# Gathered rows of the routed experts: spreads issued by SyncE six tiles ahead, lists loaded twelve ahead with 32 places

## The chip, the core and the metric

The kernel runs on one core of one Trainium2 chip. The metric is the device time of one execution in microseconds (us). Timed three times, the kernel before took 3968.76 us in the median (3964.9 to 3973.75). The core has five engines with an instruction stream each: TensorE (PE, matrix products), VectorE (DVE), ScalarE (ACT), GpSimd (POOL) and SyncE (SP). They meet at semaphores. 16 DMA engines move data for all of them.

## The reference

Two layers are chained, and the input is added at the end. The first is a modulated linear layer on 8 x 1024 rows of 512 (8192 tokens). The second is a feed-forward layer with a shared part (512 to 1024 to 512) and a routed part. The routed part is what the change touches:

```
topk_idx, w = _route(xf, router_w, e_bias)      # 8 of 64 experts for each token
order = argsort(topk_idx.reshape(-1)); tok = order // K
sorted_x = xf[tok]                               # 65536 rows, grouped by expert
g = ragged_dot(sorted_x, gate_w, group_sizes)    # [512 x 256] of the expert of the row
u = ragged_dot(sorted_x, up_w, group_sizes)
o = ragged_dot(silu(g) * u, down_w, group_sizes) # [256 x 512]
routed = zeros.at[tok].add(o * w)                # weighted and added into the token's row
out = x + shared + routed                        # x is the layer's first input
```

## The kernel before

A first phase (to about 1460 us) computes the linear layer, the shared part and the routing for all tokens. It writes the rows to be gathered into `y_rows` in DRAM, lists of (row, weight) for each expert, and a table with one entry per routed tile.

The second phase is a loop over routed tiles. A tile is 128 (token, expert) pairs of one expert; there are 532 tiles here, four to a turn of the loop (`UN = 4`). An expert's weights are a set of three DMAs of 512 KB: gate, up and down. Only the first tile of an expert brings a set, by a branch on a bit of the table. An expert takes from one tile to some dozens, and experts are ordered so that a small one stands beside a large one. Every product is made of three in fp32r (high x high, high x low, low x high), so weights and activations are split into a high and a low part: ScalarE makes the high, VectorE the low.

What happens to tile j, and on which engine:

- SyncE loads its list (`load_list`, a 1 KB DMA; `lists` has 16 places in turn) and, with `weights`, its expert's set.
- VectorE copies the row numbers out of the list (`rows_from`, tile j+8 in step j).
- GpSimd gathers 128 rows by an indirect DMA (`gather`, tile j+7 in step j) into `x_rows`, and later adds the result rows to the output by an indirect DMA (`scatter`, tile j-3 in step j, behind the gather of its step).
- ScalarE issues the "spread" of a pair of tiles (`spread`, in even steps, pair j+4, j+5): four DMAs of 128 KB that rearrange `x_rows` into `x_split`, from which a 32 x 32 transpose gives the columns that TensorE needs. Both buffers hold two pairs.
- VectorE transposes (`turn_x`, tile j+3 in step j), ScalarE and VectorE split (`x_high`, `x_low`), TensorE computes gate and up (line 1231), then turns the hidden rows of tile j-1 (line 1240), and computes down of tile j-2 (line 1249).
- ScalarE scales and copies the result out (`weigh`, first thing in step j, tile j-3). With `start_weights` and `end_weights` it makes the high parts of a new set for tile j+2 in step j; VectorE makes the low parts (`weights_low`) behind it, in steps j and j+1.

Each engine takes its instructions in the order in which the code is written, so a wait holds all that stands behind it. SyncE loads the list of tile n and then the set of tile n-4. What paces it is the 16 places: `load_list(n)` waits for the scatter of tile n-16 to have landed. It thus has nothing in front of a set but one list. The DMAs of SyncE and of ScalarE go out on a queue each, those of GpSimd on a third.

The sets have four places each (`RAW`, `RING`), and a set's issue waits for the set before it to have landed (`raw_gu_ld`, `raw_d_ld`, lines 1132 to 1135).

Of the kernel before, what the change touches and what calls it, by code (L numbers as in the profile page):

```python
# [16 lines left out]
P = 128  # L17
# [15 lines left out]
def build(nc, x, cond, cw, cbias, aff_w, aff_b, router_w, e_bias, gate_w, up_w, down_w,  # L33
          sh_gate, sh_up, sh_down, out):
    B, L, C = x.shape
    N = B * L
# [15 lines left out]
    UN = 4  # L52
# [20 lines left out]
    with top:  # L73
# [950 lines left out]
        with ExitStack() as tmp:  # L1024
# [6 lines left out]
            raw = [sb("raw_gu", [P, RAW, KC, 2 * H]), sb("raw_d", [P, RAW, KH, C])]  # L1031
            wgu = [sb("w_gu_h", [P, RING, KC, 2 * H], F32R, LINE), sb("w_gu_l", [P, RING, KC, 2 * H], F32R, LINE)]
            wdn = [sb("w_dn_h", [P, RING, KH, C], F32R, LINE), sb("w_dn_l", [P, RING, KH, C], F32R, LINE)]
            LISTS = 16
            lists = sb("lists", [P, LISTS, 2], I32)
            from_row = [sb(f"from_row{n}", [P, 1], I32) for n in range(UN)]
            to_row = [sb(f"to_row{n}", [P, 1], I32) for n in range(UN)]
# [29 lines left out]
            PARTS = [(True, 0, KC // 2 + 1), (True, KC // 2 + 1, KC), (False, 0, KH)]  # L1067
            NTURN = MAXT // UN
            assert MAXT % UN == 0 and NTURN > 2
            AHEAD = UN  # L1070

            def field(eng, j, f, top_val):

# [33 lines left out]
            @blk.sync  # L1107
            def _(sp):
                sp.dma_start(trow[:], table.rearrange("(a j) f -> a (j f)", a=1)).then_inc(tab_ld, 16)
                sp.wait_ge(tab_ld, 16)  # L1110

                def load_list(j, u, g):
                    known = isinstance(j, int)
                    if not known or j >= UN:
                        sp.wait_ge(list_ld[u], 16 * g)
                    if not known or j >= LISTS:
                        sp.wait_ge(added[u], 16 * (g - (LISTS // UN - 1)))
                        sp.nop(nofuse=True)
                    off = field(sp, j, 0, LROWS - P)
                    sp.dma_start(entry(j, 0, 2), slots[bass.ds(off, P), :]).then_inc(list_ld[u], 16)  # L1120

                def weights(j, is_first):

                    with sp.If(is_first > 0):
                        order = field(sp, j, 1, E)
                        e = field(sp, j, 2, E - 1)
                        half = order & (RAW - 1)
                        sp.wait_ge(split, 3 * order + 1)
                        sp.nop(nofuse=True)
                        if not isinstance(j, int) or j > 0:  # L1130

                            sp.wait_ge(raw_gu_ld, 32 * order)
                            sp.nop(nofuse=True)
                            sp.wait_ge(raw_d_ld, 16 * order)
                            sp.nop(nofuse=True)
                        for n, w in enumerate((gate_w, up_w)):
                            sp.dma_start(raw[0][:, bass.ds(half, 1), :, n * H:(n + 1) * H].rearrange("p a k n -> p (a k) n"),
                                         w[bass.ds(e, 1)].rearrange("e (k p) h -> p (e k) h", p=P)).then_inc(raw_gu_ld, 16)
                        sp.dma_start(raw[1][:, bass.ds(half, 1), :, :].rearrange("p a k n -> p (a k) n"),
                                     down_w[bass.ds(e, 1)].rearrange("e (k p) h -> p (e k) h", p=P)).then_inc(raw_d_ld, 16)  # L1140

                def step(g, u, is_first):
                    n = g * UN + u
                    load_list(n, u, g)
                    weights(n - AHEAD, is_first)

                for n in range(UN):
                    load_list(n, n, 0)
                    if n == 1:
                        weights(0, field(sp, 0, 3, 1))  # L1150
                for n in range(UN, 2 * UN):
                    load_list(n, n - UN, 1)
                for n in range(1, UN):
                    weights(n, field(sp, n, 3, 1))
                for n in range(2 * UN, LISTS):
                    load_list(n, n % UN, n // UN)
                    weights(n - AHEAD, field(sp, n - AHEAD, 3, 1))
                last_turn = field(sp, 0, 5, NTURN - 1)
                sp.wait_ge(words, 1)
                with sp.Fori(LISTS // UN, NTURN + 2) as g:  # L1160
                    with sp.If(last_turn >= g - 2):
                        turn = Turn(sp, g - 1)
                        for u in range(UN):
                            step(g, u, turn.first(u))
                for u in range(UN):
                    sp.wait_ge(list_ld[u], 16 * last_turn + 48)
                    sp.nop(nofuse=True)

            @blk.gpsimd
            def _(pool):  # L1170
# [24 lines left out]

                def step(g, u):
                    j = g * UN + u
                    gather(g + 1 + (u + 3) // UN, (u + 3) % UN)
                    if not isinstance(j, int) or j >= 3:
                        scatter(j - 3, (u - 3) % UN, g - 1 if u < 3 else g)  # L1200

                pool.wait_ge(tab_ld, 16)
                for n in range(UN + 3):
                    gather(n // UN, n % UN)
                for u in range(UN):
                    step(0, u)
# [7 lines left out]
                for u in range(1, UN):  # L1214
                    scatter(UN * last_turn + u, u, last_turn)
                for u in range(UN):
                    pool.wait_ge(x_ld[u], 16 * last_turn + (48 if u < 3 else 32))
                for u in range(UN):
                    pool.wait_ge(added[u], 16 * last_turn + 16)

# [61 lines left out]
            def _(act):  # L1282
# [49 lines left out]
                def spread(j, v, g):  # L1332

                    for u in (2 * v, 2 * v + 1):
                        act.wait_ge(x_ld[u], 16 * (g + 1))
                        act.nop(nofuse=True)
                    if not isinstance(j, int) or j >= UN:
                        act.wait_ge(dve_turned, j - 2)
                        act.nop(nofuse=True)
                    for a in range(QD):  # L1340
                        act.dma_start(x_split[v][a * SQ:(a + 1) * SQ, :, :, :].rearrange("c i u e -> c (i u) e"),  # L1341
                                     xg[v][:, :, a * P:(a + 1) * P]).then_inc(x_moved[v], 16)

                def step(g, u, turn):
                    j = g * UN + u
                    known = isinstance(j, int)
# [7 lines left out]
                        h_high(j - 1, (u - 1) % UN)  # L1354
                    with act.If(turn.first(u + 2) > 0):
                        end_weights(turn.order(u + 2))
                    if u % 2 == 0:
                        spread(j + UN, u // 2, g + 1)

                spread(0, 0, 0)  # L1360
                spread(2, 1, 0)
                act.wait_ge(words, 1)
                start_weights(None, 0)
                end_weights(0)
# [24 lines left out]
            def _(dve):  # L1389
# [85 lines left out]
                turn_x(1, 1, 0)  # L1475
                x_low(1, 1)
                turn_x(2, 2, 0)
                turn = Turn(dve, 0)
                with dve.If(turn.first(1) > 0):
                    weights_low(turn.order(1), (0,))  # L1480
# [40 lines left out]
```

## Time and profile before

| | |
|---|---|
| median of three timed runs | 3968.76 us |
| profiled execution: its time / its span | 3965.72 us / 3964.0 us |
| PE busy | 3733.3 us, 94% of the span, x17024 |
| DVE / ACT / POOL busy | 2235.7 / 1495.3 / 1946.4 us |
| mean granted TensorE clock | 0.977 of full speed |
| routed stretch, 1500 to 3964 us | DMA engines 0.87 busy |

The profile shows one execution. Its time outside the span is 1.7 us. A line of a timeline gives the start in microseconds from the beginning of the span, the length, the engine (SPq and ACTq are the instruction queues of SyncE and ScalarE, where DMAs are issued), the line of the program and what it writes and reads. The chain of waits is followed back from the last instruction, each piece being what released the next. The clock column is the mean of two levels, 1 being 2.4 GHz and 0.5 being 1.2 GHz.

### The profile page before, as it was taken

The page shows a single profiled execution, that of the slowest core. Times are in us where ns is not written, and L with a number is a line of the kernel's source. Part 1 is how long each engine was busy: PE and PEld are TensorE (multiplying, and loading weights), DVE is VectorE, ACT ScalarE, POOL GpSimd, SP SyncE. Part 2 cuts the span into 40 slices and gives each one's busy share as a digit, 9 for nine tenths or more (in the row PEclk, how much of TensorE's full clock was granted, in tenths as well). Part 3 has the DMA queues.
Part 4 walks back from the last instruction along what each step waited for, and adds up shares of the span by engine and source line. Part 5 has one row for each costly group of instructions (what it writes and reads, how often), then busy time and mean ns, then how long its engine had stood idle before and what let it go on. Part 6 is the DMA issues. An engine that isn't in the chain of part 4 may idle for free.

```text
span 3964.0 us, 91393 instructions
## 1 busy us (share of the span) xinstructions
PE 3733.3 (94%) x17024; PEld 3040.4 (77%) x17025; DVE 2235.7 (56%) x4612; ACT 1495.3 (38%) x3339; POOL 1946.4 (49%) x1601
## 2 busy tenths in 40 slices
PE   7999999999999959999999999999999999999987
PEld 5877877878787848878878878787878778777775
DVE  4655555555555645555555555555555555566554
ACT  3222222222222214444444444444444444444443
POOL 1453333333333425655556556555656555555554
PEclk9999999999999979999999999999999999999998
DMA  5121112112111228888889888988888898899887
GB/s 181 51 57 44 44 54 54 44 44 65 44 44 54 44 70 181 182 196 177 177 191 184 182 189 182 200 176 188 178 190 185 187 201 175 194 204 204 198 185 158
DMA packets 589051, 550.56 MB, mean 139 GB/s; under 512 B 133625, under 2 KB 443265, under 8 KB 588929
## 3 DMA queue, kind: packets, MB, share of 16 engines
q0 software_dynamic: 136112, 281.38, 36.5%
q10 hardware_dynamic: 291584, 140.58, 13.9%
q1 hardware_dynamic: 161234, 127.04, 11.7%
q8 instruction: 70, 1.15, 0.2%
q14 instruction: 51, 0.42, 0.1%
HBM read 229.07 MB, written 179.19 MB: 103 GB/s over the span
## 4 chain that ended last, share of the span: by engine, by line
PE 46%; DMA 7%; issue 4%; ACTq 3%; DVE 2%; SPq 1%; DVEq 1%; ACT 1%; POOLq 0%; POOL 0%
PE bank L1231 30%; PE bank L1249 14%; DMA x_split<-x_rows 4%; PE bank L1240 2%; ACTq L1341 2%; DMA raw_d<-in_L_ffn_down_w_dram 1%; DMA out_dram<-o_rows,to_row 1%; DVE w_dn_l L30 1%; DMA lists<-slot_list 1%; DMA x_rows<-y_rows,from_row 1%; DVE x_cols L1407 0%; ACTq L1074 0%; SPq L1074 0%; ACT x_h L1289 0%; DVE w_gu_l L30 0%
## 5 line engine op out<-in xcount | busy, mean ns | idle before, releaser
L1193 POOL DMA_INDIRECT out_dram<-o_rows,to_row x532 | 879.5, 1653 | 278.2 <-issue 230.0
L1177 POOL DMA_INDIRECT x_rows<-y_rows,from_row x539 | 543.9, 1009 | 840.6 <-DMA x_split<-x_rows 605.5
L428 POOL DMA_INDIRECT slot_list<-ent,pos x512 | 503.9, 984 | 862.7 <-PE bank L454 385.4
L1231 PE MATMUL bank<-w_gu_h,x_h 128*128 x2128 | 844.3, 397 | 86.1 <-DVE x_l L30 42.7
L1231 PE MATMUL bank<-w_gu_h,x_l 128*128 x2128 | 840.3, 395 | 0.0
L1231 PE MATMUL bank<-w_gu_l,x_h 128*128 x2128 | 839.7, 395 | 0.0
L1407 DVE STREAM_TRANSPOSE x_cols<-x_split 128x512 f32<-128x512 f32 x535 | 580.1, 1084 | 293.9 <-DMA x_split<-x_rows 293.2
L1414 DVE TENSOR_TENSOR e_hf<-bank,e_sg 128x256 f32<-128x256 f32 x532 | 225.2, 423 | 684.4 <-ACT e_sg L1295 366.2
L1231 PEld LDWEIGHTS bank<-w_gu_h,x_h 128*128 128x128 f32 x2128 | 406.4, 191 | 186.4 <-issue 99.1
L1249 PE MATMUL bank<-w_dn_h,e_h_h 128*128 x1064 | 468.1, 440 | 33.7 <-DVE e_h_l L30 20.5
L1231 PEld LDWEIGHTS bank<-w_gu_l,x_h 128*128 128x128 f32 x2128 | 406.9, 191 | 86.7
L1231 PEld LDWEIGHTS bank<-w_gu_h,x_l 128*128 128x128 f32 x2128 | 406.7, 191 | 86.9
L1249 PE MATMUL bank<-w_dn_h,e_h_l 128*128 x1064 | 425.6, 400 | 0.0
L1249 PE MATMUL bank<-w_dn_l,e_h_h 128*128 x1064 | 424.1, 399 | 0.0
L1309 ACT COPY to_row<-lists 128x1 int32 (+1 forms) x532 | 102.7, 193 | 842.9 <-issue 657.4
L30 DVE TENSOR_TENSOR x_l<-x_cols,x_h 128x512 fp32r<-128x512 f32 x534 | 368.7, 690 | 46.4 <-issue 12.7
L1289 ACT CAST x_h<-x_cols 128x512 fp32r<-128x512 f32 x534 | 329.4, 617 | 103.9 <-DVE x_cols L1407 94.9
L1310 ACT ACTIVATE o_rows<-bank,lists 128x512 f32<-128x512 f32 x532 | 366.9, 690 | 0.0
L1295 ACT ACTIVATE e_sg<-bank 128x256 f32<-128x256 f32 x532 | 202.9, 381 | 404.0 <-PE bank L1231 362.8
L1249 PEld LDWEIGHTS bank<-w_dn_h,e_h_h 128*128 128x128 f32 x1064 | 202.7, 190 | 67.5 <-issue 43.8
L742 DVE TENSOR_TENSOR stage_d<-bank,sg 128x512 f32<-128x512 f32 x128 | 88.5, 692 | 277.1 <-PE bank L454 261.9
L656 ACT ACTIVATE sg<-bank 128x512 f32<-128x512 f32 x128 | 76.5, 598 | 428.4 <-PE bank L454 376.5
(242 smaller groups left out, 5946.7 us busy)
## 6 DMA issues: line engine op xcount, KB each, us to landing
x_split<-x_rows ACTq DMA_DIRECT2D x1072, 128.0 KB
xin<-in_x_dram SPq DMA_DIRECT2D x16, 1024.0 KB
y_rows<-yrow SPq DMA_DIRECT2D x64, 256.0 KB
stage_d<-in_x_dram SPq DMA_DIRECT2D x16, 1024.0 KB
out_dram<-stage_d SPq DMA_DIRECT2D x16, 1024.0 KB
raw_gu<-in_L_ffn_gate_w_dram SPq DMA_DIRECT2D x29, 512.0 KB
raw_gu<-in_L_ffn_up_w_dram SPq DMA_DIRECT2D x29, 512.0 KB
raw_d<-in_L_ffn_down_w_dram SPq DMA_DIRECT2D x29, 512.0 KB
```

Source lines behind the costliest of these rows:

```text
L30: return nc.vector.tensor_tensor(out, full, high.bitcast(F32), ALU.subtract)
L428: nc.gpsimd.indirect_dma_start(slots, bass.IndirectOffsetOnAxis(ap=pos[v][:, t, k:k + 1], axis=0), ent[v][:, t, k, :], None).then_inc(scat ...
L1177: nc.gpsimd.indirect_dma_start(xg[u // 2][:, u % 2, :], None, y_rows, bass.IndirectOffsetOnAxis(ap=from_row[u][:].bitcast(U32), axis=0)).t ...
L1193: nc.gpsimd.indirect_dma_start(out, bass.IndirectOffsetOnAxis(ap=to_row[u][:].bitcast(U32), axis=0), og[u][:], None, compute_op=ALU.add).t ...
L1231: last = nc.tensor.matmul(b_gu[u % 2][:], xp[a][:, u % 2, k, :], wgu[b][:, bass.ds(place, 1), k, :].rearrange("p a n -> p (a n)"), start=( ...
L1249: last = nc.tensor.matmul(b_o[u % 2][:], hp[a][:, u % 2, k, :], wdn[b][:, bass.ds(place, 1), k, :].rearrange("p a n -> p (a n)"), start=(k ...
L1289: nc.scalar.copy(xp[0][:, u % 2, :, :], x_cols[:]).then_inc(act_x, 1)
L1295: nc.scalar.activation(sg[:, u % 2, :], b_gu[u % 2][:, 0:H], ACT.Silu).then_inc(act_gu, 1)
L1309: nc.scalar.copy(to_row[u][:], entry(j, 0, 1))
L1310: nc.scalar.activation(og[u][:], b_o[u % 2][:], ACT.Copy, scale=entry(j, 1, 2).bitcast(F32)).then_inc(act_do, 1)
L1407: nc.vector.transpose(x_cols[:].rearrange("p k (c i) -> p k i c", i=QD), x_split[u // 2][:, :, u % 2, :].rearrange("p i (k r) -> p k i r", ...
L1414: nc.vector.tensor_tensor(hf[:, u % 2, :], b_gu[u % 2][:, H:2 * H], sg[:, u % 2, :], ALU.mult).then_inc(dve_gu, 1)
```

## The change

Four things are moved in the routed phase. SyncE instead of ScalarE issues the spreads, in even steps, of pair j+6, j+7 instead of j+4, j+5. They stand in front of the list of that turn. SyncE's steps are numbered anew: in step j it issues the spread, the list of tile j+12 (was n, beside set n-4, so 4 tiles between the two; now 6) and the set of tile j+6. `lists` has 32 places instead of 16. GpSimd gathers tile j+8 instead of j+7 in step j, and VectorE copies the row numbers of tile j+9 instead of j+8. The transfers, the arithmetic and the buffers of rows are the same.

```diff
-            LISTS = 16
+            LISTS = 32
-            AHEAD = UN
+            LIST_AHEAD, SPREAD_AHEAD, LOAD_AHEAD = 12, 6, 6
@@ SyncE
+                def spread(j, v, g):
+
+                    for u in (2 * v, 2 * v + 1):
+                        sp.wait_ge(x_ld[u], 16 * (g + 1))
+                        sp.nop(nofuse=True)
+                    if not isinstance(j, int) or j >= UN:
+                        sp.wait_ge(dve_turned, j - 2)
+                        sp.nop(nofuse=True)
+                    for a in range(QD):
+                        sp.dma_start(x_split[v][a * SQ:(a + 1) * SQ, :, :, :].rearrange("c i u e -> c (i u) e"),
+                                     xg[v][:, :, a * P:(a + 1) * P]).then_inc(x_moved[v], 16)
-                def step(g, u, is_first):
-                    n = g * UN + u
-                    load_list(n, u, g)
-                    weights(n - AHEAD, is_first)
+                def step(g, u, turn):
+                    j = g * UN + u
+                    if u % 2 == 0:
+                        spread(j + SPREAD_AHEAD, (u + SPREAD_AHEAD) % UN // 2, g + (u + SPREAD_AHEAD) // UN)
+                    load_list(j + LIST_AHEAD, (u + LIST_AHEAD) % UN, g + (u + LIST_AHEAD) // UN)
+                    weights(j + LOAD_AHEAD, turn.first(u + LOAD_AHEAD - UN))
@@ GpSimd
-                    gather(g + 1 + (u + 3) // UN, (u + 3) % UN)
+                    gather(g + 2, u)
@@ ScalarE
-                    if u % 2 == 0:
-                        spread(j + UN, u // 2, g + 1)
@@ VectorE
-                    rows_from(j + 2 * UN, u, g + 2)
+                    rows_from(j + 2 * UN + 1, (u + 1) % UN, g + 2 + (u + 1) // UN)
```

The first tiles, before the loop, are written out anew to match: SyncE issues the first three spreads between its first lists and sets.

SyncE, in the loop over turns, one odd and one even step (before): `lists` and `raw_gu`, `raw_d` are the list and the set.

```order
L1124 UNCONDITIONAL_BRANCH
L1074 ISA
L1074 TENSOR_LOAD trow
L1074 ISA x2
L1120 REGISTER_ALU
L1120 ISA
L1120 DMA lists<-slot_list 128x2
L1124 REGISTER_ALU x2
L1124 COMPARE_AND_BRANCH
L1074 ISA
L1074 TENSOR_LOAD trow
L1074 ISA x3
L1074 TENSOR_LOAD trow
```

The same place in the kernel after, from the end of an odd step on:

```order
L1137 UNCONDITIONAL_BRANCH
L1129 REGISTER_ALU
L1132 DMA x_split<-x_rows 32x8x128 x4
L1074 ISA
L1074 TENSOR_LOAD trow
L1074 ISA x2
L1121 REGISTER_ALU
L1121 ISA
L1121 DMA lists<-slot_list 128x2
L1137 REGISTER_ALU x2
L1137 COMPARE_AND_BRANCH
```

The four spread DMAs now stand between the branch over one set and the next list, on the queue that carries the sets.

ScalarE, end of an even step of the loop, before (`e_h_h` is the hidden part's high half, `o_rows` the result rows of the next step):

```order
L1329 ISA
L1315 ISA
L1315 COPY w_dn_h<-raw_d 128x1024
L1355 UNCONDITIONAL_BRANCH
L1341 DMA x_split<-x_rows 32x8x128 x4
L1306 ISA
L1309 REGISTER_ALU
L1309 ISA
L1309 COPY to_row<-lists 128x1
L1310 ISA
L1310 ACTIVATE o_rows<-bank,lists 128x512
```

and after:

```order
L1342 COPY w_gu_h<-raw_gu 128x512
L1356 ISA
L1342 ISA
L1342 COPY w_dn_h<-raw_d 128x1024
L1370 UNCONDITIONAL_BRANCH
L1333 ISA
L1336 REGISTER_ALU
L1336 ISA
L1336 COPY to_row<-lists 128x1
L1337 ISA
L1337 ACTIVATE o_rows<-bank,lists 128x512
```

The spread has gone from between the set's casts and the next step's `to_row` and `o_rows`.

## Rows read from the trace of the kernel before

**Rows 1.** Windows: engines busy (x instructions), PEclk, DMA share, GB/s, by stretch

```profile
1500.00:3964.00 2464.00, 2342.04 (x10518) 1894.12 (x10516) 1414.90 (x2715) 1096.72 (x2718) 1406.86 (x1057) 0.98 0.87 187
...
1739.26:1776.00 36.74, 28.57 (x121) 22.02 (x120) 20.91 (x37) 17.78 (x38) 18.35 (x13) 0.95 0.95 230
...
2539.00:2551.00 12.00, 12.00 (x58) 9.81 (x57) 6.22 (x12) 6.17 (x16) 6.98 (x5) 1.00 1.06 275
```

**Rows 2.** Windows of line 1231 alone (gate and up products), same stretches

```profile
1500.00:3964.00 2464.00, 1546.44 (x6300) 1199.90 (x6300) 0.98 0.87 187
...
1739.26:1776.00 36.74, 17.60 (x72) 13.47 (x72) 0.95 0.95 230
2510.53:2573.25 62.72, 37.23 (x145) 28.60 (x145) 0.92 0.92 212
```

**Rows 3.** Chain of waits, 2084 to 2111: start, length, what

```profile
2084.11 2.73 PE bank L1231 x12
...
2097.11 2.73 PE bank L1231 x12
```

**Rows 4.** Timeline of SyncE, 1715 to 1756: start, length, instruction

```profile
1715.06 21.08 SPq L1120 DMA_DIRECT2D lists<-slot_list  x6
1739.77 0.40 SPq L1137 DMA_DIRECT2D raw_gu<-in_L_ffn_gate_w_dram  x1
...
1750.85 0.39 SPq L1137 DMA_DIRECT2D raw_gu<-in_L_ffn_gate_w_dram  x1
...
1753.43 2.06 SPq L1120 DMA_DIRECT2D lists<-slot_list  x2
```

**Rows 5.** Timeline of SyncE, 2512 to 2580

```profile
2517.29 17.62 SPq L1120 DMA_DIRECT2D lists<-slot_list  x5
2539.46 0.01 SPq L1137 DMA_DIRECT2D raw_gu<-in_L_ffn_gate_w_dram  x1
...
2551.67 0.39 SPq L1137 DMA_DIRECT2D raw_gu<-in_L_ffn_gate_w_dram  x1
```

**Rows 6.** Timeline of TensorE at four places

```profile
1752.10 0.39 PE L1231 MATMUL bank<-w_gu_h,x_h 128*128 x1
...
1776.00 0.50 PE L1231 MATMUL bank<-w_gu_h,x_h 128*128 x1 [1.02 <-DVE w_dn_l L30]
...
2523.37 0.39 PE L1231 MATMUL bank<-w_gu_h,x_h 128*128 x1
...
2549.37 0.39 PE L1231 MATMUL bank<-w_gu_h,x_h 128*128 x1
```

**Rows 7.** Timeline of ScalarE, 1750 to 1778 and 2512 to 2580

```profile
1762.31 1.48 ACT L1315 CAST w_gu_h<-raw_gu  x1 [1.59 <-issue]
...
1766.88 1.48 ACT L1315 CAST w_gu_h<-raw_gu  x1
...
2518.99 2.01 ACTq L1341 DMA_DIRECT2D x_split<-x_rows  x3
...
2563.05 1.47 ACT L1315 CAST w_gu_h<-raw_gu  x1 [1.03 <-issue]
```

**Rows 8.** Chain of waits, 1735 to 1757 and 2512 to 2580

```profile
1744.89 10.33 DMA x_split<-x_rows
...
2541.13 10.23 DMA raw_d<-in_L_ffn_down_w_dram
```

**Rows 9.** Timeline of VectorE, 1750 to 1778 and 2512 to 2580

```profile
1755.24 1.08 DVE L1407 STREAM_TRANSPOSE x_cols<-x_split 128x512 f32<-128x512 f32 x1 [6.63 <-DMA x_split<-x_rows]
...
2528.23 1.07 DVE L1407 STREAM_TRANSPOSE x_cols<-x_split 128x512 f32<-128x512 f32 x1
...
2561.03 0.15 DVE L1397 COPY from_row<-lists 128x1 int32 x1 [1.89 <-DMA lists<-slot_list]
```

**Rows 10.** DMA by queue, 1500 to 3964: packets, MB, share

```profile
q1 hardware_dynamic: 112640, 44.62, 7.4%
```

**Rows 11.** Who waited for whom, 1500 to 3964: total, times, longest

```profile
DVE x_cols L1407 <- DMA x_split<-x_rows: 291.2, 214, 7.6
```

More of the change, by code:

```diff
@@ L1120, in load_list @@
                     sp.dma_start(entry(j, 0, 2), slots[bass.ds(off, P), :]).then_inc(list_ld[u], 16)
+                def spread(j, v, g):
[4 more added lines that the diff above has]
+                        sp.wait_ge(dve_turned, j - 2)
+                        sp.nop(nofuse=True)
+                    for a in range(QD):
+                        sp.dma_start(x_split[v][a * SQ:(a + 1) * SQ, :, :, :].rearrange("c i u e -> c (i u) e"),
+                                     xg[v][:, :, a * P:(a + 1) * P]).then_inc(x_moved[v], 16)
                 def weights(j, is_first):
@@ L1150, in _ @@
                         weights(0, field(sp, 0, 3, 1))
+                spread(0, 0, 0)
                 for n in range(UN, 2 * UN):
                     load_list(n, n - UN, 1)
-                for n in range(1, UN):
+                    if n == UN + 1:
+                        spread(2, 1, 0)
+                for n in range(1, LOAD_AHEAD):
                     weights(n, field(sp, n, 3, 1))
-                for n in range(2 * UN, LISTS):
+                for n in range(2 * UN, LIST_AHEAD):
                     load_list(n, n % UN, n // UN)
-                    weights(n - AHEAD, field(sp, n - AHEAD, 3, 1))
+                spread(UN, 0, 1)
+                sp.wait_ge(words, 1)
+                known = (LISTS - LIST_AHEAD) // UN
+                assert known < N * TOPK // (P * UN)
+                for g in range(known):
+                    turn = Turn(sp, g + 1)
+                    for u in range(UN):
+                        step(g, u, turn)
                 last_turn = field(sp, 0, 5, NTURN - 1)
[L1159 to L1162, printed above, removed]
+                with sp.Fori(known, NTURN) as g:
+                    with sp.If(last_turn >= g):
+                        turn = Turn(sp, g + 1)
                         for u in range(UN):
-                            step(g, u, turn.first(u))
+                            step(g, u, turn)
                 for u in range(UN):
-                    sp.wait_ge(list_ld[u], 16 * last_turn + 48)
+                    sp.wait_ge(list_ld[u], 16 * last_turn + 16 * (1 + LIST_AHEAD // UN))
+                    sp.nop(nofuse=True)
+                for v in range(UN // 2):
+                    sp.wait_ge(x_moved[v], 16 * QD * last_turn + 16 * QD * (3 - v))
                     sp.nop(nofuse=True)
@@ L1202, in _ @@
                 pool.wait_ge(tab_ld, 16)
-                for n in range(UN + 3):
+                for n in range(2 * UN):
                     gather(n // UN, n % UN)
@@ L1216, in _ @@
                 for u in range(UN):
-                    pool.wait_ge(x_ld[u], 16 * last_turn + (48 if u < 3 else 32))
+                    pool.wait_ge(x_ld[u], 16 * last_turn + 48)
                 for u in range(UN):
@@ L1330, in end_weights @@
                     weights_high(order, order & (RAW - 1), order & (RING - 1), 2)
[L1332 to L1342, printed above, removed]
                 def step(g, u, turn):
@@ L1356, in step @@
                         end_weights(turn.order(u + 2))
-                    if u % 2 == 0:
-                        spread(j + UN, u // 2, g + 1)
-                spread(0, 0, 0)
-                spread(2, 1, 0)
                 act.wait_ge(words, 1)
@@ L1477, in _ @@
                 turn_x(2, 2, 0)
+                rows_from(2 * UN, 0, 2)
                 turn = Turn(dve, 0)
```

## The prediction

> **What bounds the kernel now.** I read the windows first. Between 1500 and 3964 us the DMA engines are 0.87 busy and TensorE is busy 2342 of 2464 us [rows 1]. The same stretch with line 1231 alone has 6300 products [rows 2], 12 to a tile, so 525 tiles. The chain of waits in a quiet place has nothing in it but TensorE: 2084.11 to 2097.11 is three tiles in 13.00 us, 4.333 us each [rows 3]. 525 tiles at that pace are 2275 us, so 189 us of the stretch are lost. That is all a change to the feeding of the tiles can win.
>
> It is lost at the weight sets. Gate and up of a set are issued 28 times after 1500 us; 26 of these come in pairs whose second follows the first by 10 to 20 us. Two pairs are in rows 4 and 5. Around the first, 72 products of line 1231 (6 tiles, 26.0 us at pace) take 36.74 us; around the second, 145 (12 tiles, 52.0 us) take 62.72 us [rows 2]. Each pair loses 10.7 us, 13 pairs 139 us. The other 50 us are the last tiles and small gaps.
>
> What ends last in a pair is the spread. The one issued last at 1744.89 takes 10.33 us [rows 8], VectorE stands 6.63 us before its transpose at 1755.24 [rows 9], and in the whole stretch such waits sum to 291 us in 214 places, up to 7.6 us [rows 11]. Meanwhile the set is in flight: from 1739.77 to 1750.85, when SyncE, which waits for it, issues the next [rows 4]. That is 11.1 us (12.2 in the second pair, rows 5). The sets themselves are early: the first set's cast on ScalarE is at 1762.31, 22.5 us after its issue [rows 7]. After the second set's cast starts it takes 9.1 us until TensorE starts its tile (1766.88 to 1776.00; 10.2 in the second pair, from 2563.05 to the end of its window at 2573.25), with the low parts on VectorE ending it [rows 6, 7]. So a pair has two causes: late spread (and list, 1.89 us at 2561.03, rows 9), and casts.
>
> **The change part by part.** I call t(j) the time at which TensorE starts gate and up of tile j.
>
> Spread. Today ScalarE issues it at the end of step j for tile j+4, whose transpose is in VectorE's step j+1. SyncE will issue it for tile j+6 as soon as tile j+3 is transposed. That is t(j)+5.9: TensorE started a tile at 2523.37 and the transpose of its step ended at 2528.23+1.07 [rows 6, 9]. It is needed at t(j+3)+4.9, so it gets 12.0 us. Four issues take 2.7 (3 of them 2.01 on ScalarE, rows 7) and waking 0.3, leaving 9.0 us for the move. The 10.33 us case is then late by 1.3 us instead of 5 to 6. On its own this would take away most of the stall of a pair's first tile. In quiet stretches TensorE loses nothing now [rows 3], so nothing comes back there.
>
> ScalarE is rid of 2.7 us of issue per pair of tiles. It is busy 1097 of 2464 us [rows 1], so I count 0 (bounds 0 to 2.7 us per pair of sets).
>
> Lists. 32 places remove SyncE's wait for a scatter; 1 KB each. The list of tile j+12 is used in VectorE's step j+3, about 13 us later. It costs nothing.
>
> Sets. This is what speaks against it. SyncE's queue was paced by the scatters and ran early enough to give the first set 22.5 us (12.2 in the other pair). Now the set of tile m is issued in step m-6, behind the spread that waits for the transpose in VectorE's step. For even m: 5.9 + 3.0 for the spread + 1.7 for the list (two lists in 2.06 us, less one issue of 0.36, rows 4) + 4.1 from the list to the set (3.6 from 1736.14 to 1739.77, 4.55 from 2534.91 to 2539.46, rows 4, 5) = t(m-6)+14.7, which is t(m-2)-2.6. For odd m one more list, but a tile earlier: t(m-7)+16.4 = t(m-2)-5.3. In the second pair today it is 2539.46 against 2549.37 [rows 5, 6], t(m-2)-9.9. So sets go out 5 to 20 us later than now, and ScalarE wants gate and up of the set at about t(m-2)+2.
>
> The second set of a pair waits for the first to land: +11.1 (rows 4). Its gate and up land later by, I estimate, 6.5 us (two thirds of a set's 11.1 is 7.4; less, since TensorE stands and the tiles' own traffic thins). Then 9.1 to the start of its tile. Together t(m+1) = issue + 26.7. At pace it would be t(m-2)+13.0. The loss is 26.7-2.6-13.0 = 11.1 us for even m, 26.7-5.3-13.0 = 8.4 for odd, mean 9.75. Spread and list of the next tiles come in SyncE's order behind the second set, and they land at about the time it does, so they hide behind it. Against 10.7 that is 0.95 gained, times 13 = 12 us.
>
> Outside the pairs I give 6 us for the small gaps that follow a pair while the stream of gathers is thin, and for the two lone sets (0 to 25 by the 50 us above). Bounds of the terms: set in flight 9.5 to 13; cast to start 8 to 10.2; issue of the set up to 4.3 us (one tile) later if SyncE runs behind. 13 pairs make of each 1 us 13 us: the sum lies between -60 and +50.
>
> The queue. Of the 7.4% of DMA time on SyncE's queue [rows 10] nearly all are sets. VectorE stands for a list of 1 KB at 2561.03 while the second set, issued from 2551.67 on, has just been in flight [rows 5, 9]: a list behind a set comes late, so the queue serves about in order. The spreads now join it, and the one of pair j+8 stands behind the set of tile j+7, as counted above.
>
> The Trainium skill, page "DMA: Bandwidth & Descriptors", section "Issuing engines are not separate DMA queues", says that issuing from several engines saves only the sequencer's issue time, as all DMAs run on the same 16 engines. Taken alone, the move would then matter by the 2.7 us of issue only. The section "Queues, rings and completion order" of the same page says that SP and ACT each own a row of rings, and each ring is consumed in order while the engine goes round the rows. By this the spread loses its own turn beside a set. The trace's list behind the set speaks for the second.
>
> Sum: 3965.7 (profiled execution) - 18 = 3947.7 us. The median of the runs shown is 3.0 above it, so 3950 us.
>
> **Rivals.**
>
> A. The sets arrive in time, and only casts are left. For: TensorE's windows with a set in flight are full (2539 to 2551: 12.00 of 12 busy, DMA engines over full at 1.06, 275 GB/s, rows 1), so bytes do get through; with two queues instead of three in play a set may land in 8 rather than 11. Then a pair costs what it takes from the first cast to the start of the second set's tile, 1762.31 to 1776.00 [rows 6, 7], less two tiles at pace: 13.7-8.7 = 5.0 us. 13 x (10.7-5.0) = 74 us: 3895 us. Against: the issue at t(m-2)-2.6.
>
> B. The wait moves from the spread to the set (slower). Place: ScalarE's `start_weights` of the first set and, behind it, the second, whose issue waits for the first. It decides at one point: a pair costs 10.7 when the first set is issued at t(m-2)-3.0 (26.7-13.0-10.7). My mean is 0.95 before it. If SyncE is held longer, by a gather that lands after the transpose (`x_ld` stands in front of the set too) or by its own code, by one tile, the loss is 14.05: 13 x 3.35 = +44 us, 4010 us. For: everything now stands in one queue of instructions. Against: SyncE mostly waits now (five lists in 17.62 us, 4.3 apart, rows 5, against 1.7 when free, rows 4).
>
> C. SyncE itself becomes the bound. Four tiles are 17.3 us; two spreads 6.0, four lists 6.8, the turn's word about 1.1: 13.9. Over 17.3 each microsecond costs 131 (525 tiles in fours). One over is 4100 us. The margin is 3.4 us, a quarter.
>
> D. Nothing measurable: what the spread gives the set takes, within 8 us: 3969 us.
>
> **How the numbers follow.** The forecast, 3930 to 3960, has 0.38; A with what lies between 0.17; B 0.25; C 0.04; D 0.16. Three runs of this kernel lie 9 us apart, so about 0.2% (8 us) is what a measurement can tell from no change. Faster by more: most of the forecast (0.35) and A, 0.52. Same: D and the edge, 0.17. Slower: B, C and the rest, 0.31. The range reaches to A's price and to B's: 3890 to 4012 us; the forecast's own is 3930 to 3960.
>
> **What would show it.** Right: the wait for `x_split` before the transposes falls from 291 us to under 100; ScalarE's idle time before the cast of `w_gu_h` is ended by the DMA of `raw_gu`, 3 to 6 us a pair; a first set is issued 2 to 6 us before t(m-2); pairs lose 8 to 11 us; 4.33 us a tile between pairs; SyncE waits for VectorE's transpose. Wrong: first sets issued more than 8 us before t(m-2) (A), or after it (B); tiles over 4.4 us in quiet stretches (C); transposes still waiting 5 us in pairs.

## The result, and the profile after

The changed kernel takes 4025.35 us, the median of 4 runs (4012.24 to 4048.41); the kernel before 3969.4 us, the median of 4. The ratio is 1.0147, with a 95% interval of 1.0099 to 1.0195. It is slower by about 56 us; the forecast was 3950 us, and the range ended at 4012. The profiled execution is the slowest of the four: its span is 4046.7 us against 3964.0 before, so its sums explain 82.7 us, more than the medians differ by.

The windows of the stretch with the routed tiles, columns as in [rows 1]:

```profile
1500.00:4046.00 2546.00, 2365.96 (x10520) 1898.80 (x10518) 1418.86 (x2715) 1124.64 (x2719) 1415.22 (x1057) 0.97 0.88 181
```

TensorE has the same work in 82 us more, and is busy for 24 us more of them (2342.0 before): the last section comes back to these. What the engines waited for in it, from the waits of SyncE, then VectorE, then ScalarE (waiting line, what ended the wait, total us, times, longest):

```profile
SPq L1127 <- DMA x_rows<-y_rows,from_row: 28.2, 26, 3.9
SPq L1148 <- DMA raw_d<-in_L_ffn_down_w_dram: 12.6, 10, 3.4
SPq L1146 <- DMA raw_gu<-in_L_ffn_up_w_dram: 1.0, 2, 0.8
SPq L1119 <- DMA out_dram<-o_rows,to_row: 0.8, 1, 0.8
SPq L1130 <- DVE x_cols L1418: 0.7, 1, 0.7
```

```profile
DVE e_hf L1425 <- ACT e_sg L1322: 615.7, 332, 9.6
DVE from_row L1408 <- DMA lists<-slot_list: 203.7, 131, 3.8
```

```profile
ACT w_gu_h L1342 <- DMA raw_gu<-in_L_ffn_up_w_dram: 122.3, 26, 8.2
```

The 291.2 us before the transposes [rows 11] have gone: no wait for `x_split` is left in VectorE's list. In their place VectorE waits 203.7 us for lists of 1 KB, and ScalarE, for the first time, 122.3 us for sets. The row to read first is a small one. SyncE waits 43 us in 2546 for everything together. In the kernel before it waited for scatters:

```profile
SPq L1118 <- DMA out_dram<-o_rows,to_row: 804.5, 388, 7.2
```

An engine that issues all day and waits for nothing is itself what the others wait for. The chain of the page says the same. By engine, before:

```profile
PE 46%; DMA 7%; issue 4%; ACTq 3%; DVE 2%; SPq 1%; DVEq 1%; ACT 1%; POOLq 0%; POOL 0%
```

After, by engine and by line:

```profile
PE 20%; SPq 19%; issue 12%; DMA 10%; POOLq 1%; DVE 1%; POOL 1%; DVEq 0%; ACT 0%; another core or an unknown queue 0%; ACTq 0%
PE bank L1258 13%; SPq L1132 7%; PE bank L1276 7%; SPq L1074 5%; DMA out_dram<-o_rows,to_row 4%; SPq L1121 3%; DMA x_split<-x_rows 3%; DMA raw_d<-in_L_ffn_down_w_dram 2%; DMA x_rows<-y_rows,from_row 1%; PE bank L1267 1%; DMA lists<-slot_list 1%; SPq L1137 1%; SPq L1085 1%; SPq L1150 1%; POOLq L1074 0%
```

SyncE's timeline in a quiet place, with no set near, shows two turns of four tiles (start, length, instruction):

```profile
2663.16 2.55 SPq L1132 DMA_DIRECT2D x_split<-x_rows  x4
2668.31 2.58 SPq L1121 DMA_DIRECT2D lists<-slot_list  x2
2671.93 2.23 SPq L1132 DMA_DIRECT2D x_split<-x_rows  x4
2675.97 2.79 SPq L1121 DMA_DIRECT2D lists<-slot_list  x2
2682.52 2.11 SPq L1132 DMA_DIRECT2D x_split<-x_rows  x4
2686.01 2.17 SPq L1121 DMA_DIRECT2D lists<-slot_list  x2
2688.79 2.65 SPq L1132 DMA_DIRECT2D x_split<-x_rows  x4
2693.38 3.88 SPq L1121 DMA_DIRECT2D lists<-slot_list  x2
2701.98 1.92 SPq L1132 DMA_DIRECT2D x_split<-x_rows  x4
```

A turn begins at 2663.16, 2682.52 and 2701.98: 19.4 and 19.5 us, where TensorE needs 17.33 for four tiles. SyncE waits 0.8 us in these 39; from the end of a spread at 2665.71 to the first list at 2668.31, for instance, SyncE runs its guards and reads one field of the table. Over the stretch from 1500 to 3900 a turn is 19.2 us in the mean (18.5 median). Summed by what its instructions belong to, SyncE's 2400 us there are, for each of 125 turns:

| part of a turn | measured, us | in the prediction |
|---|---|---|
| four lists | 8.1 | 6.8, with the checks |
| four checks whether a tile brings a set | 1.9 | in the lists' 6.8 |
| two spreads (with 0.2 of waiting) | 6.9 | 6.0 |
| the sets' reads and issues, spread over all turns | 1.0 | not counted |
| the turn's word | 0.75 | 1.1 |
| the loop's own branches | 0.64 | not counted |
| sum | 19.2 | 13.9 |

The checks belong to the lists in the prediction, because its 1.7 us a list is the pitch from one list to the next [rows 4], and a check that finds no set lies between those two.

Then the sets. One pair, from SyncE's timeline:

```profile
2584.73 0.68 SPq L1150 DMA_DIRECT2D raw_gu<-in_L_ffn_gate_w_dram  x1
...
2595.28 0.39 SPq L1150 DMA_DIRECT2D raw_gu<-in_L_ffn_gate_w_dram  x1
```

TensorE's timeline (in brackets the idle time ahead and what ended it):

```profile
2584.01 0.40 PE L1258 MATMUL bank<-w_gu_h,x_h 128*128 x1
...
2588.47 0.39 PE L1258 MATMUL bank<-w_gu_h,x_h 128*128 x1
...
2593.97 0.44 PE L1267 MATMUL bank<-ident,e_hf 128*128 128x128 f32 x2 [2.62 <-DVE e_hf L1425]
2597.26 0.79 PE L1276 MATMUL bank<-w_dn_h,e_h_h 128*128 x1 [2.86 <-DVE e_h_l L30]
...
2601.49 0.79 PE L1258 MATMUL bank<-w_gu_h,x_h 128*128 x1 [1.30 <-DVE w_dn_l L30]
```

ScalarE's and VectorE's:

```profile
2591.61 1.47 ACT L1342 CAST w_gu_h<-raw_gu  x1 [6.21 <-DMA raw_gu<-in_L_ffn_up_w_dram]
...
2601.68 1.47 ACT L1342 CAST w_gu_h<-raw_gu  x1 [4.86 <-DMA raw_gu<-in_L_ffn_up_w_dram]
```

```profile
2593.49 0.42 DVE L1425 TENSOR_TENSOR e_hf<-bank,e_sg 128x256 f32<-128x256 f32 x1 [6.31 <-ACT e_sg L1322]
...
2596.33 0.15 DVE L1408 COPY from_row<-lists 128x1 int32 x1 [1.73 <-DMA lists<-slot_list]
```

The first set's tile starts at 2601.49; its set was issued at 2584.73, 0.7 us after the tile two ahead had started (2584.01). ScalarE stands 6.21 us for it with the current tile's `e_sg` behind the cast, VectorE stands for `e_sg` and then 1.73 us for a list. The tile at 2588.47 takes 13.0 us, and with the two behind it (next starts 2611.20 and 2617.28) the pair costs 15.8.

I split the time that TensorE loses against 4.333 us a tile, from the start of the first tile to that of the last, into what is lost around the sets (from four tiles before the first set's to three after the second's, 13 pairs and the lone set of tile 526) and the rest, in each profiled execution. It is used in the table after the experiments. From before to after: around sets 150.8 to 175.5 us, elsewhere 9.4 to 67.3. The sum rises by 82.6, and the spans differ by 82.7.

### The profile page after: what moved, and what is told of

It reads as the page before. It is cut to its first block, busy times and chain, and to the rows that moved or that the text cites. A ratio compares the mean times of both kernels' runs of the same rounds, so it can differ in the third digit from the quotient of the medians.

```text
span 4046.7 us, 92175 instructions
## 1 busy us (share of the span) xinstructions
PE 3757.7 (93%) x17024; PEld 3044.6 (75%) x17025; DVE 2239.1 (55%) x4613; ACT 1523.0 (38%) x3339; POOL 1959.2 (48%) x1602
## 4 chain that ended last, share of the span: by engine, by line
PE 20%; SPq 19%; issue 12%; DMA 10%; POOLq 1%; DVE 1%; POOL 1%; DVEq 0%; ACT 0%; another core or an unknown queue 0%; ACTq 0%
PE bank L1258 13%; SPq L1132 7%; PE bank L1276 7%; SPq L1074 5%; DMA out_dram<-o_rows,to_row 4%; SPq L1121 3%; DMA x_split<-x_rows 3%; DMA raw_d<-in_L_ffn_down_w_dram 2%; DMA x_rows<-y_rows,from_row 1%; PE bank L1267 1%; DMA lists<-slot_list 1%; SPq L1137 1%; SPq L1085 1%; SPq L1150 1%; POOLq L1074 0%
## 5 line engine op out<-in xcount | busy, mean ns | idle before, releaser
L1204 POOL DMA_INDIRECT x_rows<-y_rows,from_row x540 | 554.3, 1027 | 898.3 <-DMA x_split<-x_rows 517.4
L1267 PE MATMUL bank<-ident,e_hf 128*128 128x128 f32 x1064 | 204.2, 273 | 38.6 <-DVE e_hf L1425 31.7
L1276 PEld LDWEIGHTS bank<-w_dn_h,e_h_l 128*128 128x128 f32 x1064 | 204.7, 192 | 46.3
```

Source lines behind the costliest of these rows:

```text
L1204: nc.gpsimd.indirect_dma_start(xg[u // 2][:, u % 2, :], None, y_rows, bass.IndirectOffsetOnAxis(ap=from_row[u][:].bitcast(U32), axis=0)).t ...
L1267: last = nc.tensor.transpose(b_h[u % 2][:, k * P:(k + 1) * P], hf[:, u % 2, k * P:(k + 1) * P], ident[:])
L1276: last = nc.tensor.matmul(b_o[u % 2][:], hp[a][:, u % 2, k, :], wdn[b][:, bass.ds(place, 1), k, :].rearrange("p a n -> p (a n)"), start=(k ...
```

## The experiments

Theory 1: the changed kernel is held by SyncE's own issuing time. The rivals: sets go out too late in the program (B of the prediction); 1 KB lists come late because they share a queue with sets of 1.5 MB and spreads; the early spread itself is of no use. Which theory is number 2 or 3 differs from one expectation to the next; each says it.

**One more read on SyncE.** The changed kernel with

```diff
                     if u % 2 == 0:
                         spread(...)
+                    field(sp, j, 0, LROWS - P)
                     load_list(j + LIST_AHEAD, ...)
```

> The kernel after, with one more read of a table field on SyncE in each step of its loop (value not used), about 1 us by the trace of after (13 reads of a field with their asserts take about 12.5 us). Theory 1 (SyncE's own instructions are the bound: a turn of four tiles took 19.2 us in the mean from spread to spread in the trace of after, and 17.3 us is TensorE's pace): four more us a turn come in full, 131 turns, +350 to +600 us, about 4450 us. Theory 2 (the weight sets are issued too late, in SyncE's order behind the spread): SyncE has slack between, and only the sets move, by up to 4 us a pair: +20 to +60 us, about 4060. Theory 3 (the lists land late because they stand behind 512 KB of spread in one queue): nearly no change, since the order in the queue is the same: 0 to +40.

4237.65 us (4223.42 to 4246.36), ratio 1.0687 [1.0647, 1.0728]. The turn grew from 19.2 to 20.7 us; 131 turns make of 1.5 us 197 us, and 212 were measured. One read a tile that nobody uses costs 212 us (5.4% by the ratios): this is the bound. The time lies outside all three ranges, between theory 1's (350 us and more) and those of theories 2 and 3 (at most 60). Theory 1 had the mechanism and too high a size: the four reads take 3.8 us of a turn in this trace, but the lists beside them take less than they did (6.8 instead of 8.1), and so do the checks. Why they do isn't shown.

**The lists on ScalarE.** The changed kernel, SyncE with spreads and sets only:

```diff
@@ SyncE, step
-                    load_list(j + LIST_AHEAD, (u + LIST_AHEAD) % UN, g + (u + LIST_AHEAD) // UN)
@@ ScalarE, end of the step
+                    load_list(j + LIST_AHEAD, (u + LIST_AHEAD) % UN, g + (u + LIST_AHEAD) // UN)
```

> The kernel after, with the lists of the loop loaded by ScalarE at the end of its step (12 ahead as before) instead of by SyncE, so SyncE has spreads and sets only. Theory 1: SyncE is rid of some 9 us a turn and has room again; the small losses between the pairs go (about 80 us) and the sets go out earlier: 3900 to 3960 us. Theory 2: SyncE's steps still start with the wait for the transpose, the sets are as late as now: pairs still lose 10 to 11 us, about 3960 to 3990. Theory 3: the lists have a queue of their own, VectorE's wait for lists (204 us) goes, about 3950 to 3990. Theories 1 and 3 are told apart by the first kernel of this call.

3899.01 us (3896.58 to 3903.38), ratio 0.9846 [0.9817, 0.9875]: better than both kernels, by the ratios 1.5% under the kernel before and 3.0%, 119 us, under the changed one, at the lower edge of theory 1's range. SyncE's waits:

```profile
SPq L1127 <- DMA x_rows<-y_rows,from_row: 622.9, 219, 6.0
SPq L1148 <- DMA raw_d<-in_L_ffn_down_w_dram: 25.4, 12, 3.9
SPq L1130 <- DVE x_cols L1424: 21.1, 35, 1.7
```

SyncE now waits 623 us for gathered rows. The sets stand behind that wait, but it costs nothing that earlier sets would give back: further down they go out earlier, and nothing is gained. VectorE's wait for lists is gone, its wait for `x_split` is 11.9 us, ScalarE's for sets 41.2. So the change without the load of the lists on SyncE is worth 61 us over the kernel before. Spreads and sets still share a queue here, and GpSimd and VectorE keep their new order, so none of these is what cost the changed kernel its time. How much of the 61 us is the earlier spread and how much is ScalarE's relief from issuing it was not separated.

**Only the 32 places,** in the kernel before:

```diff
-            LISTS = 16
+            LISTS = 32
```

> The kernel before with 32 places for lists instead of 16 and nothing else. SyncE is then no longer held by scatters of 16 tiles back and issues sets as early as their four places allow. If late sets or late lists are part of what a pair of sets costs in the kernel before, it is faster, by up to 3 us a pair (3930 us); if the late spread is what costs, no change: 3969 within 8 us.

3974.23 us (3966.37 to 3985.17), ratio 1.0028 [1.0011, 1.0046]. The places alone give nothing. Sets then go out some 88 us ahead of the tile two before theirs, and the tiles lose 186 us in sum instead of 160 (the profiled span is only 9 us longer, as its first routed tile starts 15 us earlier), so sets that are early in flight are no gain by themselves.

**The spread early, but from ScalarE,** the kernel before with 32 places and

```diff
-                    if u % 2 == 0:
-                        spread(j + UN, u // 2, g + 1)
+                    if u % 2 == 1:
+                        spread(j + 5, (u + 5) % UN // 2, g + (u + 5) // UN)
@@ GpSimd
-                    gather(g + 1 + (u + 3) // UN, (u + 3) % UN)
+                    gather(g + 2, u)
```

> The kernel before with 32 places for lists and the spreads still issued by ScalarE, but one step earlier: at the end of odd step k for the pair k+5, k+6 (was: even step j, pair j+4, j+5), with the gathers one tile earlier to match. It has the earlier spread without any load on SyncE and without the shared queue. If the early spread is worth something and SyncE's load is what spoilt it (theory 1), a pair loses 5 to 8 us instead of 10.7: 3895 to 3940 us. If the earlier spread gives nothing because the casts and the sets bound a pair anyway: 3969 within 8 us.

3983.19 us (3976.51 to 3993.43), ratio 1.0057 [1.0037, 1.0078]. The transposes' wait falls to 27.6 us, but not the time: it is 0.3% over that of the 32 places alone and above both expected ranges. One place of ScalarE's timeline shows what stands against the gain:

```profile
1962.09 0.37 ACT L1304 CAST e_h_h<-bank 128x256 fp32r<-128x256 f32 x1
1966.64 2.70 ACTq L1344 DMA_DIRECT2D x_split<-x_rows  x4
1971.14 0.19 ACT L1312 COPY to_row<-lists 128x1 int32 x1 [8.69 <-DMA lists<-slot_list]
```

ScalarE has nothing running from 1962.5 until it issues the spread at 1966.64, since the spread stands behind the gathers' semaphores; then come 2.70 us of issue, and the tile's own `to_row` and `o_rows` stand behind both. The engine named in brackets is only the last semaphore in line. How much of ScalarE's waiting before `to_row` is of this kind was not summed, so the price of it is argued from this place.

**Giving SyncE its load back without the lists.** The kernel with the lists on ScalarE, with two reads on SyncE before each tile's check for a set:

```diff
+                    field(sp, j, 0, LROWS - P)
+                    field(sp, j, 0, LROWS - P)
                     weights(j + LOAD_AHEAD, turn.first(u + LOAD_AHEAD - UN))
```

> The kernel e2 (lists loaded by ScalarE) with two unused reads of a table field on SyncE ahead of every tile's weight step. This gives SyncE back about the time that the lists took, with no list in its queue. Theory 1 (the changed kernel is held by SyncE's own issuing time): eight reads at about 1 us put 8 us on a turn of four tiles that e2 leaves with 622.9 us of idle waiting over 131 turns (4.8 us a turn); SyncE's turn goes to 18.5 to 19.5 us again, its waits for gathers go under 60 us, and the time to 4000 to 4060 us. Theory 2 (the lists cost because they stand in one queue with the sets and spreads, not because of SyncE's time): 3890 to 3910 us, as e2.

3974.27 us (3965.8 to 3992.66), ratio 1.0012 [0.9993, 1.003]. SyncE's queue holds what it held without the reads, so the 1.66% between the two ratios, 66 us, are SyncE's time alone. That is under theory 1's 4000 to 4060 us and far over theory 2's 3890 to 3910. SyncE's waits for gathers are 49.2 us, as expected, but the point where its time becomes the bound is only just reached. A read took 0.87 us here, so the eight take 7 us of a turn and not 8, and SyncE's own time rises by 5.2 us, as the other instructions again take less.

**Sets two tiles earlier,** first with the lists on ScalarE, then in the changed kernel itself (the turn's word is then read a turn further ahead, which the lines leave out):

```diff
-            LIST_AHEAD, SPREAD_AHEAD, LOAD_AHEAD = 12, 6, 6
+            LIST_AHEAD, SPREAD_AHEAD, LOAD_AHEAD = 12, 6, 8
-                    weights(j + LOAD_AHEAD, turn.first(u + LOAD_AHEAD - UN))
+                    weights(j + LOAD_AHEAD, turn.first(u))
```

> The kernel e2 with the expert sets issued for the tile eight ahead instead of six. The set's slot must still be free (its guard is kept), so the issue comes earlier only where the slot is. Theory 1: of the losses left in e2, the 41.2 us that ScalarE waits for sets go, and the pairs of sets lose less: 3860 to 3895 us. Theory 2 (the sets wait for their slot, not for their place in SyncE's program): no change, 3893 to 3905 us, and the waits of SyncE at the guard of the slot grow.

> The changed kernel with the expert sets issued for the tile eight ahead instead of six, lists still on SyncE. Theory 1 (SyncE's own time is the bound): SyncE's steps do not get shorter, so the turn stays at 18.5 us or more; only the lateness of sets that comes from SyncE's delay goes: ScalarE's 122.3 us of waits for sets shrink, those of VectorE for lists (203.7 us) stay, and the time is 3990 to 4030 us. Theory 2 (what costs in the changed kernel is that sets go out too late in the program, as rival B has it): the gain is most of the 56 us that the change lost and more, 3920 to 3970 us.

With the lists on ScalarE: 3912.42 us (3904.64 to 3916.9), ratio 0.9852 [0.983, 0.9874], no gain, and above both expected ranges. Both theories fail: the sets do leave earlier, 15.3 us before the tile two ahead instead of 6.4, and ScalarE's 41.2 us for them go, but VectorE's wait for `x_split` rises from 11.9 to 52.6 us. In the changed kernel: 4018.58 us (4017.54 to 4031.91), ratio 1.0115 [1.0093, 1.0137], which can't be told from the changed kernel's. This one settles rival B. First sets leave 16.6 us before that tile instead of 0.6, ScalarE's wait for them falls from 122.3 us to 1.8, and the tiles around the sets lose 179.9 us as against 175.5. ScalarE's and VectorE's waits in it:

```profile
ACT w_gu_h L1342 <- DMA raw_gu<-in_L_ffn_up_w_dram: 1.8, 2, 1.0
ACT x_h L1316 <- DVE x_cols L1418: 95.2, 41, 7.2
```

```profile
DVE from_row L1408 <- DMA lists<-slot_list: 279.9, 112, 8.5
```

ScalarE's wait for sets has gone, 120 us. VectorE's for lists has grown by 76, and ScalarE's for VectorE's transposes by 68 (27.6 in the changed kernel).

**Lists four tiles earlier,** the changed kernel with

```diff
-            LIST_AHEAD, SPREAD_AHEAD, LOAD_AHEAD = 12, 6, 6
+            LIST_AHEAD, SPREAD_AHEAD, LOAD_AHEAD = 16, 6, 6
```

> The changed kernel with the lists loaded by SyncE sixteen tiles ahead instead of twelve; SyncE does the same work in the same order. In the changed kernel VectorE waited 203.7 us for lists. Theory 1 (SyncE's issuing time per turn is the bound, and the waits for lists, sets and rows only show who notices it): the waits for lists shrink to under 100 us, those for gathered rows, casts or sets grow in their place, the turn stays at 18.5 us or more, and the time at 4010 to 4040 us. Theory 2 (lists land too late since each stands behind 1.5 MB of a set in SyncE's queue): the 203.7 us go, the time is 3930 to 3985 us.

4051.69 us (4038.76 to 4055.52), ratio 1.0188 [1.0162, 1.0213], a little above theory 1's range and far from theory 2's. VectorE's and ScalarE's waits:

```profile
DVE x_cols L1418 <- DMA x_split<-x_rows: 208.0, 102, 4.6
```

```profile
ACT to_row L1336 <- DMA out_dram<-o_rows,to_row: 217.9, 125, 4.0
ACT to_row L1336 <- PE bank L1276: 169.0, 203, 3.4
ACT w_gu_h L1342 <- DMA raw_gu<-in_L_ffn_up_w_dram: 157.4, 26, 10.5
```

The 203.7 us for lists are gone, and 208.0 for spreads stand there. A list that lands late behind a set is thus not the cause either. Three kernels (the changed one, with earlier sets, with earlier lists) give SyncE the same work for a turn and take about the same time; only the buffer that is waited for differs.

**One read and three,** in the kernel with the lists on ScalarE:

```diff
+                    field(sp, j, 0, LROWS - P)            # once, or three times
                     weights(j + LOAD_AHEAD, turn.first(u + LOAD_AHEAD - UN))
```

> The kernel e2 (lists loaded by ScalarE) with one unused read of a table field on SyncE per tile, 4 of some 0.9 us in a turn of four tiles, where SyncE waits 4.8 us a turn in e2. Theory 1 (SyncE costs nothing until its own time per turn reaches TensorE's, then all of the excess): 3895 to 3915 us, half or less of the step to e5 (3974 us with two reads). Theory 2 (every instruction on SyncE costs its time, whatever the others do): half of the step between e2 and e5, 3930 to 3945 us.

> The kernel e2 with three unused reads of a table field on SyncE per tile. Theory 1 (past the knee each read costs what it cost on top of the changed kernel, 212 us for one per tile): 4140 to 4200 us; two reads and then a third would stand on either side of the changed kernel (4025 us), whose lists are then worth between two and three reads a tile. Theory 2 (a read costs what it cost between e2 and e5, 37 us): 4000 to 4030 us.

One: 3939.63 us (3926.64 to 3943.5), ratio 0.9901 [0.9879, 0.9924]. Three: 4200.72 us (4185.26 to 4208.12), ratio 1.0562 [1.0532, 1.0592]. Three reads cost what theory 1 said, at the upper edge of its 4140 to 4200 us, and nothing like theory 2's 4000 to 4030. One read is a miss for theory 1: 3939.63 us lies outside its 3895 to 3915 and inside theory 2's 3930 to 3945.

These and the two reads' run stand beside different runs of the kernel before, so I compare ratios: 0.9846, 0.9901, 1.0012, 1.0562. The first read costs 0.55%, the second 1.11%, the third 5.50%, or 22, 44 and 218 us. The third stands far out. The first and the second can't be told apart by their intervals, so below the bound the runs are no evidence against an even price; and the first isn't free, though SyncE still waits:

```profile
SPq L1127 <- DMA x_rows<-y_rows,from_row: 266.4, 171, 6.3
```

The table puts the kernels in the order of SyncE's own time for a turn (mean turn, less its share of waits). Beside it: how far ahead of the tile two before its own the first set of a pair is issued (median), what TensorE loses around sets and elsewhere in the profiled execution, and the ratio to the kernel before:

| kernel | SyncE's own, us a turn | set ahead by | lost around sets | elsewhere | ratio |
|---|---|---|---|---|---|
| before (spreads on ScalarE) | 11.9 | 12.0 | 150.8 | 9.4 | 1 |
| lists on ScalarE | 12.9 | 6.4 | 98.7 | 5.6 | 0.985 |
| the same, sets eight ahead | 12.9 | 15.3 | 89.9 | 14.7 | 0.985 |
| one read | 15.9 | 3.8 | 120.5 | 23.5 | 0.990 |
| two reads | 18.1 | 2.6 | 147.5 | 37.1 | 1.001 |
| after, sets eight ahead | 18.6 | 16.6 | 179.9 | 47.9 | 1.012 |
| after, lists sixteen ahead | 18.7 | -2.5 | 199.9 | 41.1 | 1.019 |
| after | 18.9 | 0.6 | 175.5 | 67.3 | 1.015 |
| three reads | 20.1 | -3.5 | 238.2 | 151.5 | 1.056 |
| after with one read | 20.5 | -1.2 | 214.8 | 229.7 | 1.069 |

From the kernel with the lists on ScalarE on, two ranges can be told apart. Up to about 18 us SyncE has time over in the mean, 5.2 us more of its own time cost 1.7%, and that is mostly around the sets: 49 of the 80 us of loss between that kernel and the one with two reads. From two reads to three, 2.0 us more cost 5.5%, 109 us for each microsecond, and from the changed kernel to the one with one more read 1.6 us cost 212, or 132 for each, near the 131 turns. The loss elsewhere grows fast there. The three kernels with the lists on SyncE fall between those with two and three reads in their own time and in their ratio; there is no sign that a list costs anything beyond SyncE's time for it.

## Why the prediction was wrong

The step that failed is rival C's sum, "two spreads 6.0, four lists 6.8, the turn's word about 1.1: 13.9", with "the margin is 3.4 us, a quarter". The measured turn is 19.2 us where TensorE needs 17.33, so there was no margin. Most of the gap is the lists with their checks, 10.0 us and not 6.8: their pitch was read off one pair, 2.06 us long [rows 4], one of the short ones. Pairs in the lines above take 2.17 to 3.88, and in the kernel before the pitch of two lists is 2.2 us in the mean of 368 once the waits are taken out, where I took 1.7. The spreads were 0.9 too low (their 0.3 us for waking stood in no row; from the end of the wait to the first issue it is 0.2 us in the median in the kernel with the lists on ScalarE). The sets' reads and issues, 1.0, and the loop's branches, 0.64, were not in the sum at all.

The trace of the kernel before had the number. From 1500 to 3900 us a turn of SyncE is 18.5 us in it, of which 6.6 are waits, so 11.9 are its own, for the lists, checks, word, sets and loop. The prediction's sum has 7.9 for them. With the measured 6.9 for two spreads, 11.9 makes 18.8, and 18.9 was measured.

The price, "Over 17.3 each microsecond costs 131", is about right for what is added beyond that point (109 and 132 us for each, as above). "One over is 4100 us" is not: it adds the price to a kernel that already loses 160 us, and 1.6 over would be 4175 by it, where 4025 was measured.

From this follow the others, in order.

- The spread: right. The stall before the transposes went, 291 us to none. The kernel with the lists on ScalarE shows what the change can bring: 52 us less around the sets than before, 4 less elsewhere.
- "It costs nothing", of the lists: wrong, and the dearest of the steps. Moving them off SyncE, with nothing else changed, gives 119 us. The reason given, 13 us of lead for a 1 KB transfer, looks at the transfer and not at who issues it.
- The sets: predicted at 2.6 or 5.3 us before the tile two ahead, measured at 0.6 (between 2.6 before and 1.6 after, 14 first sets). ScalarE's wait for the DMA of `raw_gu` did appear, 26 times and 122.3 us, 9.4 a pair instead of 3 to 6. A pair loses 12.9 us in the mean of the 13, and 11.1 before (the 10.7 came from two of them), where I had said 9.75: +24 us and not -12. My formula with the measured 0.6 gives 26.7-0.6-13.0 = 13.1. That agreement is luck: with the sets leaving 16.6 us ahead a pair still loses 13.0.
- Outside the pairs: -6 us was forecast, within 0 to -25 by the gaps that were there. The loss away from all sets rose by 58 instead, from 9.4 to 67.3. The "other 50 us" held less than I took them to: some 28 of them lie behind the start of the last tile. This is the largest term of the loss, and its range I had closed at zero on that side: by "In quiet stretches TensorE loses nothing now" nothing could come back, but something could come.
- Rival B had the sign and nearly the size (4010), and its sign in the trace nearly came true: 5 of the 14 first sets are issued after t(m-2). It is still not the cause: with the sets 16 us earlier the loss around them is 179.9 us instead of 175.5, and the time is the same.
- Rival C had the cause and a chance of 0.04. It should have carried most of what B had.
- "Against: SyncE mostly waits now" was the trap. The 4.3 us pitch of lists before was a wait for scatters, 804.5 us in the stretch; but the change adds two spreads a turn and puts them under the same roof as everything else, and how long SyncE can wait says how much room there is only after the new instructions are in the sum: 6.6 us a turn waited before, less 6.9 for the spreads.

The Trainium skill's page "DMA: Bandwidth & Descriptors", section "Issuing engines are not separate DMA queues", leaves the issuing engine's own time as all that several issuing engines save, and calls it usually small beside the DMA. I had set that aside as a matter of "2.7 us of issue only" and given the case to the order in the queue. The runs agree that it is the issuer's time that counts: unused reads, which put nothing into any queue, cost 22 to 218 us. Small it was not here: the spreads' 6.9 us a turn are more than a third of the 17.33 that TensorE needs.

What stays open: whether a cheaper program on SyncE with the lists kept (fewer reads of the table, no check where no set can be) does as well as moving them. That wasn't tried. Open too is why SyncE's instructions take less each when reads are added. Nor is it shown which part of the first read's 22 us, paid while SyncE still waits in the mean, acts through sets and which through spreads after a pair.

## What to carry to other kernels

Before work is moved onto an engine that only issues, add up that engine's whole loop: every DMA it starts, every field it reads, every check that is not taken, the loop itself, each at the pitch measured where it is not waiting, and compare it with the pace of the busiest engine. When three different buffers arrive late at once and the issuer's waits are near zero, don't lengthen their leads: the wait only changes its name. Put cheap loads on an engine that has room, and a wait that can be long on one with nothing urgent behind it.

## What the runs showed of the hardware

- Four DMA instructions of a spread keep SyncE 2.6 us in the mean (1.9 to 3.5) and ScalarE 2.70 in the line above, one of a 1 KB list about 0.36 us. A read of a field from a table in SBUF, with its range checks, took 0.87 us, more than starting either. A list with its guards and its read is 2.0 us of SyncE. These times are not fixed prices: with one more read a tile the lists took 1.7 us each.
- TensorE stood 2.62 us before 2593.97 and again for 2.86 us before 2597.26. At 2595.60, within the second, its granted clock went to the lower of its two levels, 1.2 GHz. The windows of 2595.60 to 2605.84 and, for comparison, of a full tile, columns as in [rows 1]:

```profile
2595.60:2605.84 10.24, 7.28 (x16) 5.28 (x17) 5.91 (x8) 5.38 (x11) 0.00 (x0) 0.50 0.83 205
2584.01:2588.47 4.46, 4.46 (x21) 3.58 (x20) 1.70 (x4) 0.81 (x2) 3.56 (x3) 1.00 0.68 156
```

  A product took 0.63 us in the first (2597.85) instead of 0.39. Over the profiled run the granted clock was 0.967 (0.977 before, 0.981 with the lists on ScalarE, 0.961 with one more read). From 1500 us on the lower level holds for 164 us, and for 113 before. The 24 us that TensorE is busy longer for the same work are, as I read them, the part of the 82 us that this makes; the rest is idle time.
